# Half-width sums, aggregate and residual, an earlier copy of the context's spectrum, and products placed ahead of a subtraction in a two-layer attention kernel

## The reference

```
x = x + L0_xattn(layernorm(x), ctx)      # autocorrelation attention
x = x + L0_ffn(layernorm(x), ...)        # base matrix + 2 of 8 low-rank experts
x = x + L1_xattn(layernorm(x), ctx, ...) # windowed attention, 8 heads, window 16
x = x + L1_ffn(layernorm(x), ...)        # 2 of 4 low-rank experts

# L0_xattn, for each of the 8 heads, along the 128 positions:
qf = fft(q); kf = fft(k)
corr = ifft(qf * conj(kf)).real
w, idx = top_k(corr, 9);  w = softmax(w)
out[l] = sum_i w_i * v[min(idx_i + l, 127)]
```

## Time and profile before

| what | value |
|---|---|
| median of 3 runs | 1845.26 us (1844.0 to 1845.53) |
| the profiled execution: its time | 1846.75 us |
| the profiled execution: its span | 1845.0 us |
| TensorE busy | 1704.8 us (92%) |
| VectorE busy | 1567.8 us (85%) |
| ScalarE busy | 1130.9 us (61%) |
| GpSimd busy | 892.9 us (48%) |

### The profile page before, as it was taken

The page is one execution under the profiler, slowest core; times in us unless marked ns, Lnnn a source line. Parts: engine busy times, 40 slices in busy tenths (PEclk is TensorE's granted clock), DMA queues, the critical chain, the costliest instruction groups (busy, mean ns, idle before and its releaser), DMA issues.

```text
span 1845.0 us, 48106 instructions
## 1 busy us (share of the span) xinstructions
PE 1704.8 (92%) x19296; PEld 1082.1 (59%) x19296; DVE 1567.8 (85%) x4726; ACT 1130.9 (61%) x1929; POOL 892.9 (48%) x869
## 2 busy tenths in 40 slices
PE   4689999999999999999999999999999999999975
PEld 2356566666556666556666655666665566666553
DVE  6778898889889888988888988988898898888853
ACT  5257656666656665665666666666566566667542
POOL 2345544455554545554455555454555545455432
PEclk7899999999999999999999999999999999999995
DMA  6033322343332233332233343223433322333220
GB/s 217 28 58 70 58 49 48 56 70 70 69 46 48 50 68 70 70 59 51 49 53 69 70 70 52 50 51 59 70 70 59 55 48 50 70 70 59 24 36 24
DMA packets 549359, 111.37 MB, mean 60 GB/s; under 512 B 531088, under 2 KB 531344, under 8 KB 548624
## 3 DMA queue, kind: packets, MB, share of 16 engines
q1 hardware_dynamic: 549136, 108.30, 31.5%
HBM read 57.94 MB, written 16.78 MB: 40 GB/s over the span
## 4 chain that ended last, share of the span: by engine, by line
PE 57%; DVE 20%; ACT 10%; POOL 7%; issue 6%; DMA 0%; DVEq 0%; SPq 0%; POOLq 0%; ACTq 0%
PE pb L602 18%; PE pc L677 8%; ACT q_diag L876 6%; PE pa L561 4%; POOL prob L1419 4%; PE pa L523 3%; ACT v_im L776 3%; PE pa L495 3%; PE pa L524 3%; PE pa L496 3%; PE pa L497 3%; PE pb L591 3%; DVE rows_c L1248 2%; DVE x_c L1138 2%; POOL rest L1419 2%
## 5 line engine op out<-in xcount | busy, mean ns | idle before, releaser
L602 PE MATMUL pb<-w_base_h,even_words 128*128 128x512 f16 x1024 | 324.8, 379 | 0.0
L1426 POOL TENSOR_TENSOR p_hl<-sc,p_hl 128x512 f16<-128x512 f32 x128 | 164.3, 1284 | 220.5 <-ACT p_hl L776 220.5
L1453 POOL TENSOR_TENSOR sc<-sc,sc_rec 128x512 f32<-128x512 f32 x128 | 134.1, 1048 | 262.0 <-DVE sc_rec L1235 262.0
L876 ACT ACTIVATE q_diag<-sc,own 128x512 f32<-128x512 f32 x384 | 244.3, 710 | 3.1 <-DVE sc L1146 3.1
L602 PE MATMUL pb<-w_base_l,even_words 128*128 128x512 f16 x512 | 193.9, 379 | 0.0
L486 PE MATMUL pa<-xn_a,tab 128*128 128x512 f32 x384 | 181.3, 609 | 3.8 <-ACT xn_a L776 3.8
L677 PEld LDWEIGHTS pc<-sc_t,v_diag 128*128 128x128 f16 x6144 | 170.2, 97 | 20.6 <-DVE sc_t L1242 5.9
L677 PE MATMUL pc<-sc_t,v_diag 128*128 128x32 f16 x6144 | 173.9, 177 | 5.5 <-DVE sc_t L1242 5.5
L655 PE MATMUL pc<-k_h,q_diag 128*128 128x32 f16 x2048 | 168.8, 177 | 0.0
L656 PE MATMUL pc<-k_l,q_diag 128*128 128x32 f16 x2048 | 168.3, 177 | 0.0
L657 PE MATMUL pc<-k_h,q_diag 128*128 128x32 f16 x2048 | 168.3, 177 | 0.0
(11 more groups left out here) (165 smaller groups left out, 4649.5 us busy)
## 6 DMA issues: line engine op xcount, KB each, us to landing
x_a<-in_x SPq DMA_DIRECT2D x32, 512.0 KB, 5.5
x_res<-in_ctx_in SPq DMA_DIRECT2D x32, 512.0 KB, 5.5
x_res<-in_x SPq DMA_DIRECT2D x32, 512.0 KB, 3.7
v_diag<-even_words SPq DMA_DIRECT2D x128, 128.0 KB, 4.9
v_diag<-p_hl SPq DMA_DIRECT2D x128, 128.0 KB, 4.9
out<-rows_c SPq DMA_DIRECT2D x32, 512.0 KB, 2.6
v_diag<-in_base_w SPq DMA_DIRECT2D x4, 1024.0 KB, 9.9
q_diag<-in_ra SPq DMA_DIRECT2D x1, 544.0 KB, 13.8
```

The lines of the kernel that those rows point to most:

```text
L602: mm(pb[:, h, :], rows[:, cols], weights[:, j, h * HALF:(h + 1) * HALF], start=(j == 0 and m == 0), stop=False)
L876: nc.scalar.activation(q_diag[:, blocks, head * QB:(head + 1) * QB], q_hl.rearrange("p (n t) -> p n t", t=QB)[:, blocks], ACT.Copy, scale= ...
L1426: g_.tensor_tensor(part[:, :, :, LO], sc[:, g % 2, :, :], part[:, :, :, HI], ALU.subtract)\
L1453: g_.tensor_tensor(sc[:, g % 2, :, :], sc[:, g % 2, :, :], sc_rec[:, blocks].unsqueeze(2).to_broadcast([P, GB, KEYS]), ALU.mult)\
```

## The change

There are five edits. The two sums of `a_sum` are cut into halves of 512 columns, and stand in the order: real part of the first half, imaginary part of the first half, then the second half. `a_aggregate` goes half by half in the same way, and signals after each half. `a_residual` adds half by half, each behind its own half of the aggregate. `c_router` starts when the first half of its features is there, and waits for the other after four of its eight matmuls. On ScalarE `a_values` moves ahead of two more of the second half's query blocks; on VectorE `a_product` moves ahead of `c_subtract(i - 1, 0)`.

```diff
-            def a_aggregate(b, n):
-                pe.wait_ge(sum_w.sem, sum_w.after(b, n + 1))
-                for h in range(2):
-                    last = mm(pa[:, h, :], tab[:, [AGG_RE, AGG_IM][n], :],
-                              [agg_re, agg_im][n][:, h * HALF:(h + 1) * HALF], start=(n == 0), stop=(n == 1))
-                if n == 1:
-                    last.then_inc(mm_agg.sem, 1)
+            def a_aggregate(b, h):
+                cols = slice(h * HALF, (h + 1) * HALF)
+                pe.wait_ge(sum_w.sem, sum_w.after(b, 2 * h + 1))
+                mm(pa[:, h, :], tab[:, AGG_RE, :], agg_re[:, cols], start=True, stop=False)
+                pe.wait_ge(sum_w.sem, sum_w.after(b, 2 * h + 2))
+                mm(pa[:, h, :], tab[:, AGG_IM, :], agg_im[:, cols], start=False, stop=True)\
+                    .then_inc(mm_agg.sem, 1)
...
             def c_router(b):
-                pe.wait_ge(xt_out[1].sem, xt_out[1].after(b))
                 for j in range(KT):
+                    if j % 4 == 0:
+                        pe.wait_ge(xt_out[1].sem, xt_out[1].after(b, j // 4 + 1))
...
                 if not first(b):
-                    act.wait_ge(sum_w.sem, sum_w.after(b - 1, 1))
+                    act.wait_ge(sum_w.sem, sum_w.after(b - 1, 3))
...
                     b_query_blocks(i - 2, 0, 1)
+                if live(0):
+                    a_values(i)
+                if live(2):
                     b_query_blocks(i - 2, 1, 1)
                     b_query_blocks(i - 2, 2, 1)
-                if live(0):
-                    a_values(i)
-                if live(2):
                     b_query_blocks(i - 2, 4, 1)
                     b_query_blocks(i - 2, 5, 1)
...
             def a_residual(b):
-                dve.wait_ge(mm_agg.sem, mm_agg.after(b))
                 dve.wait_ge(xres_in.sem, xres_in.after(b))
                 if not first(b):
                     dve.wait_ge(x2_out.sem, x2_out.after(b - 1))
-                v.tensor_tensor(x_b[:, :], pa_lo, x_res[:, :], ALU.add).then_inc(x1_out.sem, 1)
+                for h in range(2):
+                    cols = slice(h * HALF, (h + 1) * HALF)
+                    dve.wait_ge(mm_agg.sem, mm_agg.after(b, h + 1))
+                    v.tensor_tensor(x_b[:, cols], pa[:, h, :], x_res[:, cols], ALU.add).then_inc(x1_out.sem, 1)
...
-                if live(1):
-                    c_subtract(i - 1, 0)
                 if live(-1):
                     a_product(i + 1)
+                if live(1):
+                    c_subtract(i - 1, 0)
...
-            def a_sum(b, n):
-
-                pool.wait_ge(prod_w.sem, prod_w.after(b, n + 3))
-                g_.tensor_tensor([agg_re, agg_im][n], [agg_re, agg_im][n], [v_im, v_re][n][:, :],
-                                 [ALU.add, ALU.subtract][n]).then_inc(sum_w.sem, 1)
+            def a_sum(b, h):
+                cols = slice(h * HALF, (h + 1) * HALF)
+                pool.wait_ge(prod_w.sem, prod_w.after(b, 3))
+                g_.tensor_tensor(agg_re[:, cols], agg_re[:, cols], v_im[:, cols], ALU.add).then_inc(sum_w.sem, 1)
+                pool.wait_ge(prod_w.sem, prod_w.after(b))
+                g_.tensor_tensor(agg_im[:, cols], agg_im[:, cols], v_re[:, cols], ALU.subtract)\
+                    .then_inc(sum_w.sem, 1)
```

More of the change, by code:

```diff
@@ L312, in build @@
         prod_w = signal("prod_w", 4)
-        sum_w = signal("sum_w", 2)
-        mm_agg = signal("mm_agg")
-        x1_out = signal("x1_out")
+        sum_w = signal("sum_w", 4)
+        mm_agg = signal("mm_agg", 2)
+        x1_out = signal("x1_out", 2)
         tr_x = [signal(f"tr_x{n}", 2) for n in range(2)]
@@ L998, in step @@
                     b_query_blocks(i - 2, 0, 1)
-                    b_query_blocks(i - 2, 1, 1)
-                    b_query_blocks(i - 2, 2, 1)
                 if live(0):
@@ L1003, in step @@
                 if live(2):
+                    b_query_blocks(i - 2, 1, 1)
+                    b_query_blocks(i - 2, 2, 1)
                     b_query_blocks(i - 2, 4, 1)
@@ L1343, in step @@
                     b_norm_rows(i, 1)
+                if live(-1):
+                    a_product(i + 1)
                 if live(1):
                     c_subtract(i - 1, 0)
-                if live(-1):
-                    a_product(i + 1)
                 if live(2):
```

## The result

The changed kernel takes 1904.63 us (median of 4 runs, 1903.23 to 1905.86) against 1845.39 for the kernel before: a ratio of 1.032, with a 95% interval of 1.030 to 1.034. It is 59 us slower. The forecast was slower by 33, with a range that ends at 1890; the direction was right and the size was not.

A forecast was written before the change was run, and what follows sets the result against it. TensorE, busy for 92% of the span, was taken as the bound, so only its waits count. Per repetition 1.84 us lost and 0.63 gained, 30 x 1.2 = 36, less 3 at the edges: 1845.26 to 1878 us, range 1867 to 1890.

The forecast's parts named there:

- the whole sum: All repetitions: 1.84 us lost and 0.63 gained, 1.2 more in each of 30, 3 less at the edges: 1878 us.
- The new wait: TensorE, at the scores of group 1, waits for VectorE's late subtraction: 2.3 us, 30 times, about 70 us in all.
- The half sums: GpSimd's sums of 512 columns: 1.28 us each, bounded by 1.18 and 1.28; rival of dearer ones, 1897 us, chance 0.03.
- The router's wait: TensorE ahead of the router: the wait falls from 0.74 to about 0.25 us, which only makes room for early aggregate passes.
- VectorE waits 0.40 ahead of the first product: VectorE comes to the first product at 881.43 and waits about 0.4 us for the query's spectrum.
- the aggregate's last pass: TensorE's last aggregate pass waits about 0.4 us for GpSimd's last half sum and starts at 874.69.
- no wait is left ahead of the correlations: TensorE's wait of 0.33 us ahead of the correlations goes.
- The repetition without a fall: The distance from one repetition to the next: 55.5 us where it was 54.3.
- ScalarE's move: ScalarE's copies ahead of two query blocks: ready 1.2 us earlier, but the products wait for the query's spectrum; costed at nothing.
- The swap's own price: Products ahead of the subtraction: from the query's spectrum on, the correlations take 6.43 us instead of 4.59, 1.84 lost a repetition.
- the gain of the other four edits: The context's spectrum on TensorE starts at 877.12 instead of 877.75: 0.63 us gained a repetition.
- TensorE's clock: Rival, chance 0.04: TensorE's clock falls; held unlikely because the new wait of 2.3 us stands alone in 54 us of dense work.

The follow-up runs named there:

- the filler: Nine unread matmuls of 512 columns put into TensorE's wait for the subtraction, in the changed kernel: 1879.73 us, ratio 1.017.
- The swap: The kernel before with a single edit, the two products ahead of the subtraction: 1950.46 us; with nine unread matmuls in TensorE's wait as well, 1907.05 us.

## Why the prediction was wrong, step by step

**Right: the whole sum but the clock.** The new wait was forecast at 2.3 us and is 2.17. The half sums were put at 1.28 us between bounds of 1.18 and 1.28; the groups by form on GpSimd have them at 1.28:

```profile
L1422 POOL TENSOR_TENSOR rest<-rest,v_im 128x512 f32<-128x512 f32 x60 | 76.7, 1278 | 84.2 <-DVE v_im L1105 84.2
L1424 POOL TENSOR_TENSOR prob<-prob,v_re 128x512 f32<-128x512 f32 x60 | 76.6, 1277 | 0.0
```

The router's wait is 0.25 as forecast, VectorE waits 0.40 ahead of the first product as forecast, the aggregate's last pass waits 0.36 us where about 0.4 was forecast (it starts at 899.09, the pass before it, of 0.86 us, at 897.87), and no wait is left ahead of the correlations. The repetition without a fall lasts 55.56 us against 55.5. The whole sum was measured by itself, with the filler in the wait, at 1879.7 us against 1878.

**Terms slightly off.** ScalarE's move was costed at nothing and is worth 2.8 us where the subtraction stands first. The swap's own price, without the clock, is 2.00 us a repetition in the kernel before and 1.90 in the changed one (55.56 - 53.66), and not 1.84; the gain of the other four edits is 0.67 with the subtraction first and 0.77 behind the products (56.33 - 55.56), and not 0.63. In the changed kernel the two errors cancel: 2.00 - 0.77 = 1.23, where 1.84 - 0.63 = 1.21 was forecast. That the sum came so close is in part luck.

**Wrong: TensorE's clock, which the sum puts at nothing.** The fall was in the list of rivals with a chance of 0.04, because the new wait "is 2.3 us, but stands alone in 54 us of dense work". The only falls I had read were in the pipeline's end, behind 2.74 us and other waits close by the earlier trace rows (a 512-column matmul takes 0.61 us there and 0.38 in the earlier trace rows, and the granted clock is 0.50 from 1794.97 to 1796.80 us), and I took company to be what counts. In the runs a single wait was enough, 1.53 us 13 times in 30 and 2.17 us 16 times in 30, in repetitions that hold no other wait of over 0.4 us. I had also treated it as all or nothing: in each repetition, 54 us in all by my estimate of 1.8 us a fall, or in none. It is 1.5 us in 15 of 30 repetitions and about 1 in the first: 24 us by the starts of `x_c`, and 1879.7 + 24 = 1904, against 1904.6 measured. A chance for "in some or all of them", at 1.5 us each, would have carried the range to about 1925.

In the middle the trace of before could not exclude a fall: TensorE's longest wait there is the 0.74 us of the earlier trace rows. But it has a nearer case than that of the earlier trace rows, which I had not read to its end. Where the regular repetitions end, TensorE waits at scores for the same subtraction, for 1.60 us, and 1.3 us later the granted clock is 0.51:

```profile
1748.28 0.38 PE L649 MATMUL pc<-band_bf,ident_bf 128*128 128x512 bf16 x1 [0.88 <-ACT q_diag L876]
...
1751.45 1.09 PE L575 MATMUL pb<-ident,xn_b 128*128 128x128 f32 x8 [1.59 <-DVE xn_b L1037]
...
1755.56 0.38 PE L649 MATMUL pc<-band_bf,ident_bf 128*128 128x512 bf16 x1 [1.60 <-DVE sc L1226]
...
1756.80:1760.20 3.40, 3.40 (x57) 3.40 (x54) 2.97 (x8) 0.36 (x1) 1.33 (x2) 0.51 0.02 5
```

That wait has company too, so it could not say whether one alone is enough. It does show a fall without any wait as long as the forecast 2.3 us, and a chance of 0.04 was too low beside it.

**The best version** is the subtraction first with the other four edits: 1821.08 us, 1.4% faster than the kernel before. It loses nothing that can be measured if the router's half is left out (1821.72 us).

What stays open is what decides when the clock falls. The runs give cases (1.04 us in none of 30, 1.53 us in 13, 2.17 us in 16 or in 29, with repetitions of different length), and no run separates the wait from the light work of the scores behind it.

## What to carry to other kernels

When an instruction is moved ahead on one engine, look at what now stands behind it and which other in-order queue needs that first: here the products came early for correlations that TensorE could only reach through the scores, which waited for the delayed subtraction. Halving a producer paid where its consumer stands at its end in two passes (sums and aggregate, some 15 us by what is left of the 26), and not where the consumer waits for something else (the router, 1821.72 us against 1821.08). And a new TensorE wait of the size seen here (1.5 to 2.3 us) in an otherwise dense stream had two prices, its length (1.9 to 2.0 us a repetition behind 2.17 and 2.26) and the clock's fall (about 1.5 us each); a few matmuls that nobody reads, put into the wait, told the two apart (1904.6 us against 1879.7).

## What the runs showed of the hardware

Behind a single wait of 1.53 us TensorE's granted clock fell 13 times in 30, behind one of 1.04 us in none of 30. A fall cost about 1.5 us, and in the one shown the granted clock is 0.50 from 966.0 to 969.4 us and 1.00 from 969.6 to 972.0. More work made the kernel faster: 9 unread matmuls a repetition took it from 1904.6 to 1879.7 us. And 0.86 us more work a repetition at another place cost 43 us instead of 26; with it the clock fell 29 times in 30 and not 16.
